# Cross-attention and ternary feed-forward: exponentials, reciprocal and normalisation of a unit each one slot later

## Chip, cores, metric

One core of one Trainium2 chip. The metric is the device time of one execution in microseconds (us).

## What is computed

The input x has 8 batches of 512 rows of 512 columns, the context 120 rows for each batch. All of it is float32 at the interface. Cut to what matters:

```python
x = x + xattn(layernorm(x), ctx, mask)      # 16 heads of 32; softmax over 120 keys; masked scores are 1e-9
x = x + ffn(layernorm(x))                   # two "bitlinear" layers, 512 -> 2048 -> 512, erf GELU between

def bitlinear(x, w, b):                     # rms-normalised rows rounded to 8-bit steps of the row's maximum,
    return act_quant(rmsnorm(x)) @ weight_quant(w).T + b      # weights rounded to -1, 0, 1
```

## The kernel before

Each engine runs its own instruction list, written out by hand, and the lists are tied by semaphores; every engine takes its list strictly in order. The work is cut into **units**: one unit is one group of 4 heads by 128 rows of one batch. A batch has 16 units (number u = 4 * head group + row tile), the kernel 128 (number n). All engines loop over **slots** n = 0 to 127 with a function `slot(n)` each, and in a slot each engine does its part of several units of different ages, with attention of batch a, projections for batch a + 1 and the feed-forward part of batch a - 1.

A unit's way through the attention, before the change:

- slot n, TensorE: `scores` (L416) into one of three PSUM banks ps_s, 128 rows by 480 columns (4 heads by 120 keys). It waits until the exponentials of unit n - 3 are done.
- slot n, VectorE: `softmax_max` puts 1e-9 at masked keys (L768) and takes the negated maximum per head (L771).
- slot n, ScalarE: `exps` (L626), 4 ACTIVATEs with Exp and the maximum as bias into prob (4 buffers); each also sums its row (the ACTIVATION_READ_ACCUMULATOR records).
- slot n + 1, VectorE: `invert_sums` (L776), the reciprocal of the 4 sums. GpSimd: `normalize` (L1024), prob times the reciprocal.
- slot n + 3 (LAG = 3), TensorE: `turn_probs` (L423), four transposes into one of two banks ps_t, which waits for `normalize` and for the bank's last reader. ScalarE: `evac_probs` (L601) copies them to probT.
- every 4 units, in slots with u = 3, 7, 11, 15: TensorE's `attend` (L434) multiplies with the values into the single bank ps_a; ScalarE's `evac_o` (L612) writes the rounded part oT_h, VectorE's `oT_low` (L740) the remainder oT_l. The next user of ps_a waits for it; in slot 3 that is the output projection (L366, 12 matmuls) of the batch before, which also needs its values; in slots 8 and 0 a query projection (also L366).

The feed-forward tile k (128 rows, 32 of them) takes 4 slots. TensorE's `ffn_up` (L453) fills ps_z, one quarter a slot, and VectorE's `evac_up` (L811) empties it into hid; the next quarter waits for that. In slots with u = 2, 6, 10, 14 (from unit 26 on) ScalarE's `gelu` (L633) runs over the full hid, a slot later its `square_h` (L639), then VectorE's `h_scale` (L817 to L823), then GpSimd's `round_h` (L1031, L1034) and `h_factor`; `ffn_down` (L463) and `evac_down` (L829) end it. GELU and Exp need different tables, so an ACT_TABLE_LOAD stands before the GELU and before the next Exp. In slots 6, 7, 10 and 11 GpSimd also rounds the feed-forward input (`round_x` L993 and L998, `y_factor`, `add_b2` L1019). Slots 11 to 13 turn the next batch's normalised input (L373) through ps_t, with a cast on ScalarE (L588) and a subtraction on VectorE (L735); slots 9 and 10 project the keys and values of the next batch (L396), copied by ScalarE (L617, L621); in slot 15 VectorE spreads the keys (`spread_keys`, L758).

Batch 0 also prepares the weights. In slot 0 ScalarE rounds wo (L673) and VectorE takes the remainder (L894). Slots 1 to 6 sum absolute values of 8 pieces of the two feed-forward weights (L648, L848). Slots 8 to 15 round a piece each (VectorE L855 and L858, GpSimd L1055 and L1058), and slots 9 to 16 turn it (L490): four groups of transposes, alternately into ps_z, emptied by ScalarE (L659), and ps_y, emptied by VectorE (L869); the third and fourth group wait for the evacuation of the first and second.

The order inside ScalarE's slot before: `evac_o`, `evac_probs(n - 3)`, `exps(n)`, then weights, evacuations of projections, `square_h`, `gelu`. VectorE's: residual, `evac_down`, `softmax_max(n)`, `spread_keys`, `invert_sums(n - 1)`, `oT_low`, `evac_up`, then weights, the layer norm statistics, `h_scale`. GpSimd's: `round_x`, `round_h`, `normalize(n - 1)`, `h_factor`, weights, `add_b2`, `add_bo`, `ln1_apply`.

Of the kernel before, what the change touches and what calls it, by code (L numbers as in the profile page):

```python
# [27 lines left out]
def xattn_bitffn_kernel(nc, x, ctx_in, mask, wq, bq, wk, bk, wv, bv, wo, bo, w1, b1, w2, b2, out):  # L28
# [19 lines left out]
    NU = NB * U  # L48
# [52 lines left out]
    with ExitStack() as stack:  # L101
# [483 lines left out]
        def _(act):  # L585
# [37 lines left out]
            def exps(n):  # L623
                wait(act, "sc_max", n + 1)
                for i in range(HG):
                    last = nc.scalar.activation(prob[:, n % 4, i * S2:(i + 1) * S2],  # L626
                                                ps_s[n % 3][:, i * S2:(i + 1) * S2], ACT.Exp,
                                                bias=nmax[:, n % 4, i:i + 1], accum_out=psums[:, n % 4, i:i + 1])
                last.then_inc(s["exp_done"], 1)
# [31 lines left out]
            def slot(n):  # L661
                a, u = divmod(n, U)
                more = a + 1 < NB
                if u == 3 and a > 0:
                    evac_o(a - 1, 3)
                if u in (7, 11, 15):
                    evac_o(a, u // 4 - 1)
                if n >= LAG:
                    evac_probs(n - LAG)
                exps(n)  # L670
                if n == 0:
                    act.wait_ge(s["wo_in"], 16)
                    nc.scalar.copy(wo_h[:], stage.rearrange("p (k n) -> p k n", k=KD)).then_inc(s["wo_high"], 1)  # L673
                if n in (1, 3, 5):
                    sum_abs(n + 1)
                if WTURN <= n < WTURN + 8:
                    evac_piece(n - WTURN, 0)
                    evac_piece(n - WTURN, 2)
                if u == 7 and more:
                    evac_ctx(a + 1)  # L680
                if u == 11 and more:
                    evac_xn(a + 1, 0)
                if u == 12 and more:
                    evac_xn(a + 1, 1)
                    evac_xn(a + 1, 2)
                if u == 13 and more:
                    evac_xn(a + 1, 3)
                k = tile_at(n, SQ0)
                if k is not None:
                    square_h(k)  # L690
                if u == 0:
                    evac_q(a, 1)
                if u == 1:
                    evac_q(a, 2)
                if u == 8:
                    evac_q(a, 3)
                if u == 14 and more:
                    evac_q(a + 1, 0)
                if u == 9 and more:
                    evac_keys(a + 1)  # L700
                if u == 10 and more:
                    evac_values(a + 1)
                k = tile_at(n, GELU0)
                if k is not None:
                    gelu(k)
# [13 lines left out]
            evac_values(0)  # L719
            for n in range(NU):  # L720
                slot(n)
            for n in range(NU - LAG, NU):
                evac_probs(n)
            evac_o(NB - 1, 3)
# [5 lines left out]
        def _(dve):  # L730
# [43 lines left out]
            def invert_sums(n):  # L774
                wait(dve, "exp_done", n + 1)
                v.reciprocal(pinv[:, n % 4], psums[:, n % 4]).then_inc(s["inv_ready"], 1)  # L776
# [48 lines left out]
            def evac_down(k):  # L825
                wait(dve, "x2b2_ready", k + 1)
                wait(dve, "hdeq_ready", k + 1)
                wait(dve, "y_full", k + 1)
                v.scalar_tensor_tensor(x2[:, k % XR], ps_y[:], h_deq[:, k % T:k % T + 1], x2[:, k % XR], ALU.mult,  # L829
                                       ALU.add).then_inc(s["y_evac"], 1)  # L830
# [40 lines left out]
            def slot(n):  # L871
                a, u = divmod(n, U)
                more = a + 1 < NB
                if u in (4, 5, 6, 7) and a > 0:
                    k = T * (a - 1) + u - 4
                    wo_done(k)
                    residual(k, ps_a)
                k = tile_at(n, YOUT0)
                if k is not None:
                    evac_down(k)  # L880
                softmax_max(n)
                if u == 15 and more:
                    spread_keys(a + 1)
                if n > 0:
                    invert_sums(n - 1)
                if u == 3 and a > 0:
                    oT_low(a - 1, 3)
                if u in (7, 11, 15):
                    oT_low(a, u // 4 - 1)
                if n >= UP0:  # L890
                    evac_up((n - UP0) // FC, (n - UP0) % FC, ps_z)
                if n == 0:
                    dve.wait_ge(s["wo_high"], 1)
                    v.tensor_tensor(wo_l[:], stage.rearrange("p (k n) -> p k n", k=KD), wo_h[:].bitcast(F32),  # L894
                                    ALU.subtract).then_inc(s["wo_split"], 1)
                if n in (2, 4, 6):
                    sum_abs(n + 1)
                if n == 7:
                    weight_scales()
                if WTURN <= n < WTURN + 8:  # L900
                    evac_piece(n - WTURN, 1)
                    evac_piece(n - WTURN, 3)
                if WROUND <= n < WROUND + 8 and dve_rounds(n - WROUND):
                    round_piece(n - WROUND)
                if u in (5, 6) and a > 0:
                    ln2_scales(T * (a - 1) + u - 5)
                if u in (9, 10) and a > 0:
                    ln2_scales(T * (a - 1) + u - 7)
                k = tile_at(n, ABS0)
                if k is not None:  # L910
                    h_scale(k)
                if u == 1 and more:
                    hide(a + 1, mask_in)
                if u in (1, 2) and more:
                    ln1_stats(a + 1, 2 * u - 2)
                    ln1_stats(a + 1, 2 * u - 1)
                if u == 11 and more:
                    xT_low(a + 1, 0)
                if u == 12 and more:
                    xT_low(a + 1, 1)  # L920
                    xT_low(a + 1, 2)
                if u == 13 and more:
                    xT_low(a + 1, 3)
# [16 lines left out]
            for n in range(NU):  # L940
                if n == 2 * U - 9:
                    dve.wait_ge(s["bias_in"], 48)
                slot(n)
            invert_sums(NU - 1)
            h_scale(25)
            for c in range(1, FC):
# [25 lines left out]
        def _(pool):  # L972
# [48 lines left out]
            def normalize(n):  # L1021
                wait(pool, "inv_ready", n + 1)
                pr = prob[:, n % 4].rearrange("p (h c) -> p h c", h=HG)
                gp.tensor_tensor(pr, pr, pinv[:, n % 4].unsqueeze(2).to_broadcast([P, HG, S2]), ALU.mult  # L1024
                                 ).then_inc(s["prob_ready"], 1)
# [35 lines left out]
            def slot(n):  # L1061
                a, u = divmod(n, U)
                more = a + 1 < NB
                if u == 6 and a > 0:
                    add_bo(T * (a - 1) + 3)
                if u in (6, 7) and a > 0:
                    round_x(T * (a - 1) + u - 6)
                    y_factor(T * (a - 1) + u - 6)
                if u in (10, 11) and a > 0:
                    round_x(T * (a - 1) + u - 8)  # L1070
                    y_factor(T * (a - 1) + u - 8)
                k = tile_at(n, QH0)
                if k is not None:
                    round_h(k)
                if n > 0:
                    normalize(n - 1)
                if k is not None:
                    h_factor(k)
                if WROUND <= n < WROUND + 8 and not dve_rounds(n - WROUND):
                    round_piece(n - WROUND)  # L1080
                if u in (6, 7) and a > 0:
                    add_b2(T * (a - 1) + u - 6)
                if u in (10, 11) and a > 0:
                    add_b2(T * (a - 1) + u - 8)
                if u == 2 and a > 0:
                    add_bo(T * (a - 1))
                    add_bo(T * (a - 1) + 1)
                if u == 3 and more:
                    ln1_apply(a + 1)
                if u == 4 and a > 0:  # L1090
                    add_bo(T * (a - 1) + 2)
# [9 lines left out]
            for n in range(NU):  # L1101
                if n == U + 2:
                    pool.wait_ge(s["bias_in"], 48)
                slot(n)
            normalize(NU - 1)
            round_h(25)
            h_factor(25)
# [43 lines left out]
```

## Time and profile before

| | |
|---|---|
| median of 3 runs | 857.52 us (854.35 to 858.08) |
| the profiled execution: its own time | 861.91 us |
| its span, first to last instruction | 860.1 us |
| TensorE matmul busy | 733.6 us, 85% |
| VectorE busy | 607.4 us, 71% |
| ScalarE busy | 536.8 us, 62% |
| GpSimd busy | 508.3 us, 59% |
| mean granted TensorE clock | 0.952 of full speed |

The numbers of the table below the first line are of one profiled execution. PE is TensorE, PEld its weight loads, DVE VectorE, ACT ScalarE, POOL GpSimd, SP SyncE. A row of the timeline gives start and duration in us, engine, line, operation, what it writes and reads, and in brackets how long the engine was idle before it and for whom it waited. The chain of waits is the chain of work that ended last, followed back from the end. Times of one instruction overlap a little with the next on the same engine.

### The profile page before, as it was taken

What the parts mean: (1) busy time and instruction counts of PE and PEld (TensorE: products, weight loads), DVE (VectorE), ACT (ScalarE), POOL (GpSimd) and SP (SyncE); (2) the same over time, 40 slices, a digit from 0 to 9 for tenths busy, and PEclk for the clock granted to TensorE, in tenths of its full rate; (3) what the DMA queues carried; (4) which work ended last, traced back from release to release, by engine and by line L of the source; (5) the groups of instructions that cost most, each with busy time, mean ns of one, the idle gap of its engine ahead of it and who ended that gap; (6) DMA issues with size and microseconds to landing.
All of it is one profiled execution on the core that took longest, in us unless ns stands there. A gap on an engine that the chain in (4) does not pass through costs nothing.

```text
span 860.1 us, 10519 instructions
## 1 busy us (share of the span) xinstructions
PE 733.6 (85%) x3213; PEld 423.7 (49%) x3266; DVE 607.4 (71%) x1069; ACT 536.8 (62%) x1448; POOL 508.3 (59%) x648
## 2 busy tenths in 40 slices
PE   1857858897999899998999899989998999879764
PEld 1434445553555455645565456545554556435221
DVE  4377456676778777877797687867787759858670
ACT  2357444457767786777766776777777776764230
POOL 3025233666478547864788458864785458776852
PEclk9977989998999999999999999999999999999897
DMA  9553251001422142224212231214223211232223
GB/s 312 179 191 125 100 187 53 25 19 26 125 52 43 43 135 61 50 49 134 61 38 57 78 98 49 56 30 127 57 49 50 74 50 49 50 94 59 68 74 86
DMA packets 111840, 70.17 MB, mean 82 GB/s; under 512 B 91368, under 2 KB 91368, under 8 KB 111016
## 3 DMA queue, kind: packets, MB, share of 16 engines
q1 hardware_dynamic: 110200, 69.48, 28.6%
q8 instruction: 27, 0.44, 0.2%
q10 hardware_dynamic: 1584, 0.01, 0.1%
q14 instruction: 29, 0.24, 0.1%
HBM read 40.11 MB, written 8.39 MB: 56 GB/s over the span
## 4 chain that ended last, share of the span: by engine, by line
PE 55%; DVE 18%; ACT 13%; POOL 6%; issue 4%; DMA 3%; DVEq 0%; SPq 0%; POOLq 0%; ACTq 0%
PE ps_a L366 18%; PE ps_z L453 8%; PE ps_s L416 7%; PE ps_y L463 7%; PE ps_a L396 6%; PE ps_t L423 4%; ACT prob L626 4%; DVE ps_s L768 3%; DVE nmax L771 3%; DVE hs L817 2%; ACT L633 2%; DVE kblk L758 2%; DMA q_hT<-q_h 2%; PE ps_a L434 2%; POOL hid L1031 1%
## 5 line engine op out<-in xcount | busy, mean ns | idle before, releaser
L1024 POOL TENSOR_TENSOR prob<-prob,pinv 128x480 f32<-128x480 f32 x128 | 128.1, 1001 | 225.1 <-DVE pinv L776 224.8
L626 ACT ACTIVATE prob<-ps_s,nmax 128x120 f32<-128x120 f32 x512 | 178.4, 366 | 48.1 <-DVE nmax L771 47.7
L601 ACT COPY probT<-ps_t 120x512 f32<-120x512 f32 x128 | 75.2, 588 | 111.6 <-PE ps_t L423 111.2
L463 PE MATMUL ps_y<-w2T,q_hT 128*128 128x512 bf16 x496 | 131.1, 392 | 15.2 <-DMA q_hT<-q_h 12.1
L768 DVE COPY_PREDICATED_SCALAR ps_s<-hidden_key,masked_c 128x480 f32 x128 | 91.6, 716 | 56.0 <-PE ps_s L416 54.9
L416 PE MATMUL ps_s<-kblk,qT 128*128 128x480 f32 x256 | 129.2, 588 | 2.1 <-DVE kblk L758 2.1
L453 PE MATMUL ps_z<-w1T,q_xT 128*128 128x512 bf16 x420 | 116.6, 395 | 9.3 <-DVE hid L811 6.8
L423 PEld LDWEIGHTS ps_t<-ident,prob 128*120 128x120 f32 x512 | 63.2, 144 | 102.9 <-issue 81.4
L626 ACT ACTIVATION_READ_ACCUMULATOR prob<-ps_s,nmax 128x1 f32 x512 | 108.0, 211 | 0.0
L423 PE MATMUL ps_t<-ident,prob 128*120 128x128 f32 x512 | 83.8, 289 | 24.1 <-DVE xnT_l L735 13.5
L1031 POOL TENSOR_SCALAR hid<-hid,hs 128x2048 f32<-128x2048 f32 x32 | 63.3, 1977 | 66.5 <-DVE hs L823 53.3
L811 DVE SCALAR_TENSOR_TENSOR hid<-ps_z,y_deq,b_row 128x512 f32<-128x512 f32 x114 | 83.2, 730 | 11.7 <-PE ps_z L453 11.4
L463 PEld LDWEIGHTS ps_y<-w2T,q_hT 128*128 128x128 bf16 x512 | 47.6, 100 | 80.6 <-issue 38.9
L771 DVE TENSOR_REDUCE nmax<-ps_s 128x4 f32<-128x480 f32 x128 | 84.2, 658 | 4.4
L639 ACT ACTIVATE q_h<-hid 128x2048 bf16<-128x2048 f32 x32 | 61.6, 1926 | 26.9 <-DMA q_hT<-q_h 26.9
L817 DVE TENSOR_REDUCE hs<-hid 128x1 f32<-128x2048 f32 x32 | 72.8, 2275 | 0.0
L633 ACT ACTIVATE hid<-hid 128x2048 f32<-128x2048 f32 x32 | 61.1, 1910 | 16.7 <-DVE hid L811 16.4
L453 PEld LDWEIGHTS ps_z<-w1T,q_xT 128*128 128x128 bf16 x456 | 45.0, 101 | 41.8 <-DVE hid L811 10.0
L1034 POOL TENSOR_SCALAR q_h<-hid 128x2048 bf16<-128x2048 f32 x32 | 60.8, 1899 | 2.8
L366 PE MATMUL ps_a<-wo_h,oT_h 128*128 128x512 f32 x116 | 50.3, 433 | 11.1 <-DVE oT_l L740 10.9
L366 PE MATMUL ps_a<-xnT_h,wq_h 128*128 128x512 f32 x128 | 57.4, 448 | 2.4 <-ACT qT L607 2.4
L829 DVE SCALAR_TENSOR_TENSOR x<-ps_y,h_deq,x 128x512 f32<-128x512 f32 x32 | 24.0, 749 | 49.7 <-PE ps_y L463 49.5
(130 smaller groups left out, 1375.6 us busy)
## 6 DMA issues: line engine op xcount, KB each, us to landing
hid<-in_L_ffn_w_dram SPq DMA_DIRECT2D x10, 1024.0 KB, 5.1
xn<-in_x_dram SPq DMA_DIRECT2D x8, 1024.0 KB, 6.1
x<-in_x_dram SPq DMA_DIRECT2D x32, 256.0 KB, 3.3
out_dram<-x SPq DMA_DIRECT2D x32, 256.0 KB, 2.2
x<-in_L_ffn_w_dram SPq DMA_DIRECT2D x3, 1024.0 KB, 5.0
ctx_k<-in_ctx_dram SPq DMA_DIRECT2D x8, 240.0 KB, 3.1
ctx_k<-in_mask_Bx1xSxS_ik_dram SPq DMA_DIRECT2D x7, 240.0 KB, 3.0
x<-in_L_xattn_wq_dram SPq DMA_DIRECT2D x1, 1024.0 KB, 8.9
```

The lines of the kernel that those rows point to most:

```text
L366: last = nc.tensor.matmul(bank, w, m, start=(k == 0 and i == 0), stop=(k == KD - 1 and i == 2))
L416: nc.tensor.matmul(ps_s[n % 3][:, 0:GK], qT[:, (G * a + g) % 3, t * P:(t + 1) * P], kblk[:, g], start=True, stop=True).then_inc(s["sc_full ...
L423: last = nc.tensor.transpose(bank[0:S2, i * P:(i + 1) * P], prob[:, n % 4, i * S2:(i + 1) * S2], ident[:])
L453: last = nc.tensor.matmul(bank[:], q_xT[:, k % 3, i], w1T[:, i, c * CH:(c + 1) * CH], start=(i == 0), stop=(i == KD - 1))
L463: last = nc.tensor.matmul(ps_y[:], q_hT[:, k % 2, f], w2T[:, f], start=(f == 0), stop=(f == KF - 1))
L626: last = nc.scalar.activation(prob[:, n % 4, i * S2:(i + 1) * S2], ps_s[n % 3][:, i * S2:(i + 1) * S2], ACT.Exp, bias=nmax[:, n % 4, i:i + ...
L633: nc.scalar.activation(hid[:, k % 2], hid[:, k % 2], ACT.Gelu).then_inc(s["gelu_done"], 1)
L768: v.copy_predicated(sc, hidden_key[:, a % 2, u % T].unsqueeze(1).to_broadcast([P, HG, S2]), masked_c[:].unsqueeze(2).to_broadcast([P, HG, ...
L771: v.tensor_reduce(out=nmax[:, n % 4], in_=sc, op=ALU.max, axis=AX_X, negate=True).then_inc(s["sc_max"], 1)
L811: v.scalar_tensor_tensor(hid[:, k % 2, c * CH:(c + 1) * CH], bank[:], y_deq[:, k % 8:k % 8 + 1], b1_row[:, c * CH:(c + 1) * CH], ALU.mult, ...
L817: v.tensor_reduce(out=hs[:, 3, t:t + 1], in_=hid[:, k % 2], op=ALU.max, axis=AX_X, apply_absolute_value=True).then_inc(s["h_abs"], 1)
L1024: gp.tensor_tensor(pr, pr, pinv[:, n % 4].unsqueeze(2).to_broadcast([P, HG, S2]), ALU.mult).then_inc(s["prob_ready"], 1)
```

## The change

Exponentials of unit n move from slot n to the head of slot n + 1 on ScalarE, ahead of `evac_o` and `evac_probs`. The reciprocal moves from slot n + 1 to slot n + 2 on VectorE, ahead of `softmax_max`. The normalisation moves from slot n + 1 to slot n + 2 on GpSimd, at its old place in the slot. The transposes stay in slot n + 3. After the loop the units left over are finished.

```diff
@@ ScalarE @@
             def slot(n):
                 a, u = divmod(n, U)
                 more = a + 1 < NB
+                if n > 0:
+                    exps(n - 1)
                 if u == 3 and a > 0:
                     evac_o(a - 1, 3)
                 if u in (7, 11, 15):
                     evac_o(a, u // 4 - 1)
                 if n >= LAG:
                     evac_probs(n - LAG)
-                exps(n)
...
             for n in range(NU):
                 slot(n)
+            exps(NU - 1)
             for n in range(NU - LAG, NU):
                 evac_probs(n)
@@ VectorE @@
                     evac_down(k)
+                if n > 1:
+                    invert_sums(n - 2)
                 softmax_max(n)
                 if u == 15 and more:
                     spread_keys(a + 1)
-                if n > 0:
-                    invert_sums(n - 1)
...
                 slot(n)
+            invert_sums(NU - 2)
             invert_sums(NU - 1)
             h_scale(25)
@@ GpSimd @@
                     round_h(k)
-                if n > 0:
-                    normalize(n - 1)
+                if n > 1:
+                    normalize(n - 2)
                 if k is not None:
                     h_factor(k)
...
                 slot(n)
+            normalize(NU - 2)
             normalize(NU - 1)
             round_h(25)
```

## Rows read from the trace of the kernel before

**Rows 1.** Busy time by stretch: us, PE, PEld, DVE, ACT, POOL busy (x instructions), PEclk, DMA share, GB/s
```profile
28.00:31.00 3.00, 2.11 (x6) 0.77 (x5) 0.00 (x0) 0.69 (x1) 0.00 (x0) 1.00 0.00 0
48.00:140.00 92.00, 64.59 (x293) 41.10 (x291) 57.28 (x92) 49.65 (x166) 33.55 (x29) 0.83 0.43 148
420.06:512.27 92.21, 86.27 (x387) 49.94 (x392) 71.87 (x131) 66.07 (x180) 61.14 (x79) 0.98 0.25 68
```

**Rows 2.** Waits, whole span: engine line <- releaser: us in total, times, longest us
```profile
POOL prob L1024 <- DVE pinv L776: 224.8, 63, 31.0
...
ACT prob L626 <- DVE nmax L771: 47.7, 74, 3.8
```

**Rows 3.** Timeline, slots 2 and 3 of batch 4: start us, us, engine line [idle before]
```profile
419.05 0.58 ACT L601 COPY probT<-ps_t 120x512 f32<-120x512 f32 x1 [1.43 <-PE ps_t L423]
...
420.03 0.72 DVE L811 SCALAR_TENSOR_TENSOR hid<-ps_z,y_deq,b_row 128x512 f32<-128x512 f32 x1
...
421.56 1.28 ACT L633 ACT_TABLE_LOAD   x1
...
422.85 1.91 ACT L633 ACTIVATE hid<-hid 128x2048 f32<-128x2048 f32 x1
...
424.67 0.67 ACT L612 ACTIVATE oT_h<-ps_a,bv_col 128x512 fp32r<-128x512 f32 x1
...
425.37 0.75 DVE L740 SCALAR_TENSOR_TENSOR oT_l<-ps_a,bv_col,oT_h 128x512 fp32r<-128x512 f32 x1 [0.93 <-ACT oT_h L612]
...
426.27 0.47 PE L366 MATMUL ps_a<-wo_h,oT_h 128*128 128x512 f32 x1 [1.42 <-DVE oT_l L740]
```

**Rows 4.** Timeline, slot 15 and 0 after it
```profile
495.96 0.67 ACT L612 ACTIVATE oT_h<-ps_a,bv_col 128x512 fp32r<-128x512 f32 x1
...
498.71 0.74 DVE L811 SCALAR_TENSOR_TENSOR hid<-ps_z,y_deq,b_row 128x512 f32<-128x512 f32 x1
...
499.51 1.04 PE L453 MATMUL ps_z<-w1T,q_xT 128*128 128x512 bf16 x4
```

**Rows 5.** Timeline, slots 11 to 13
```profile
476.94 0.69 DVE L735 TENSOR_TENSOR xnT_l<-ps_t,xnT_h 128x512 fp32r<-128x512 f32 x1 [2.33 <-ACT xnT_h L588]
...
482.89 1.11 PE L423 MATMUL ps_t<-ident,prob 128*120 128x128 f32 x4 [2.09 <-DVE xnT_l L735]
```

**Rows 6.** Timeline, GpSimd in slot 7, TensorE in slot 8
```profile
451.23 0.99 POOL L1024 TENSOR_TENSOR prob<-prob,pinv 128x480 f32<-128x480 f32 x1
...
451.68 0.60 PE L423 MATMUL ps_t<-ident,prob 128*120 128x128 f32 x4
```

**Rows 7.** Timeline, last unit's reciprocal
```profile
764.52 0.18 DVE L776 RECIPROCAL pinv<-psums 128x4 f32<-128x4 f32 x1 [1.85 <-ACT prob L626]
```

**Rows 8.** Timeline, slot 10 of batch 0
```profile
89.02 0.58 ACT L617 COPY ctx_k<-ps_a 120x512 f32<-120x512 f32 x1 [4.88 <-PE ps_a L396]
...
91.28 0.36 ACT L626 ACTIVATE prob<-ps_s,nmax 128x120 f32<-128x120 f32 x1 [0.43 <-DVE nmax L771]
...
92.63 0.61 ACT L659 ACTIVATE w2T<-ps_z 128x512 bf16<-128x512 f32 x1
...
93.29 0.58 PE L490 MATMUL ps_z<-ident,hid 128*128 128x128 f32 x2 [2.20 <-ACT w2T L659]
```

**Rows 9.** Chain of waits, unit 0 and on
```profile
42.48 1.79 ACT wo_h L673
...
44.29 2.30 DVE wo_l L894
...
47.00 5.32 DMA ctx_k<-in_mask_Bx1xSxS_ik_dram
```

**Rows 10.** Chain of waits, two output projections
```profile
157.35 4.58 PE ps_a L366 x12
...
426.27 3.00 PE ps_a L366 x12
```

**Rows 11.** Timeline, the first of the two
```profile
157.35 0.47 PE L366 MATMUL ps_a<-wo_h,oT_h 128*128 128x512 f32 x1 [2.39 <-DVE oT_l L740]
```

## The prediction

> **What bounds the kernel now.** I read the busy time by stage first [rows 1]. One batch of 16 units in the middle takes 92.21 us and TensorE is busy 86.27 of them: TensorE is the bound there, and only some 6 us a batch are left in which it waits. In the stretch that turns the weights (48 to 140) TensorE is busy only 64.59 of 92.00 us: there it waits for other engines. Next the list of waits [rows 2]: the one that the change is made for, ScalarE's exponentials waiting for VectorE's negated maximum, is 47.7 us in 74 places. A wait of ScalarE is not yet time of the kernel. So I then went through the timeline of one middle batch and of the start and asked at each TensorE gap what ScalarE did before it [rows 3]. In the middle TensorE waits in few places, each time behind a short chain that runs through ScalarE: the evacuation of an attention group (L612), its low half on VectorE (L740), and then either the output projection, or the evacuation of ps_z (L811) that stands behind L740 in VectorE's queue.
>
> **The change, part by part.** No instruction is added or taken away and no DMA is moved (SyncE's queue waits for the same events as before). Exponentials, reciprocal and normalisation of a unit move one slot later. What counts is the new order in three first-in-first-out queues. On ScalarE one unit's exponentials now stand ahead of L612 and of the copy of the turned probabilities (L601). From their start to that of the next instruction it is 1.35 us (91.28 to 92.63, [rows 8]). In slots 3, 7, 11 and 15 a GELU was the last thing on ScalarE, so the load of the exponential table (1.28 us, as the GELU's own in [rows 3]) moves ahead of L612 with them: 2.8 us in all stand ahead of L612 that stood behind it.
>
> *Slot 3 (output projection, batches 2 to 7).* Before: copy 419.05, exponentials 420.06 after VectorE's maximum, table load 421.56, GELU 422.85, L612 424.67, L740 425.37, TensorE 426.27 [rows 3]. After: exponentials of the older unit lie in the 1.43 us that ScalarE waited before its copy, so the load can start at 419.64 and the GELU at 420.93; its last input starts at 420.03 and takes 0.72, so it is there. Then: load 422.86, exponentials 424.16, L612 425.52. It is 0.85 late against 424.67, though the GELU was 1.9 early. Six times: **+5.1**.
>
> *Slot 15 to 0 (six passages, from batch 1 to 2 on).* The GELU doesn't start earlier here, as a projection of TensorE ends before it, so L612, at 495.96 before, is put back by the full 2.8, to 498.73. VectorE spreads the keys meanwhile, which hides half of it: L740 0.70 later at 499.43 as in [rows 3], ps_z evacuated behind it from 500.10 instead of 498.71, and TensorE, which took ps_z at 499.51 [rows 4], is 1.4 late. Six times: **+8.4**.
>
> *Slot 11 to 12 (batches 1 to 6).* Here a chain of ScalarE's cast and VectorE's subtraction of the next input holds TensorE already; VectorE sat idle 2.33 us in it, TensorE 2.09 at its end [rows 5]. The late L612 lands in that idle time; L740 and L811 then run directly before the subtraction and put it back by 0.3. Six times: **+1.8**.
>
> *Slot 7.* L612 had waited for TensorE and the GELU is early, so it is late by 0.3 only, 3 us before anybody needs it: nothing; the cover is those 3 us.
>
> *GpSimd.* Its first wait of its own list (224.8 us for the reciprocal, [rows 2]) shrinks, which is worth nothing where it idled. But the unit that TensorE turns in slot n+1 is now normalised in slot n, behind rounding work of that slot. I compared for all 16 slots the end of the normalisation in slot n with TensorE's transposes of slot n+1: it holds by 0.6 to 4 us, except in slot 7, where GpSimd has a queue of feed-forward work without a pause: 451.23 + 0.99 is 452.22, the transposes began at 451.68 [rows 6]. Late by 0.6 with the semaphore, batches 2 to 7: **+3.6**.
>
> *Last batch.* TensorE has light slots and the chain goes through ScalarE and VectorE. The same 2.8 us in slot 11 put back VectorE's next evacuation of ps_z by 2.0; at the end two sets of exponentials, one load and the GELU lie in front of the reciprocal, which waited 1.85 for them at 764.52 [rows 7]: that one becomes some 3.8 late, and the rest of the tail hangs on it. **+3.8**. Ends: 0 to 6.
>
> *Weights being turned (units 9 to 16).* This is what the change gains. In slot 10: ScalarE copied keys at 89.02 (0.58), waited for the maximum, did exponentials at 91.28, evacuated ps_z at 92.63, and TensorE went on at 93.29 after 2.20 idle [rows 8]. After: exponentials directly at 89.60, copy 91.08, evacuation 91.67, TensorE 92.33: 0.95 earlier. The same steps in slots 9 to 16 give 1.4, 0.95, 1.0, 1.4, 1.9, 1.6, 0.2, 1.8 (in slot 15 VectorE's key spreading takes over as the limit): **-10.2**. Ends: -6 (a weight piece or GpSimd's rounding late) and -14 (no low clock).
>
> *Start.* wo had landed before 28 (no DMA traffic from 28 to 31, [rows 1]), yet its cast stood behind unit 0's exponentials and ran at 42.48, then VectorE's split 44.29, then the mask's load 47.00, which held VectorE [rows 9]. The cast now comes first, so the split can begin at 41.0: 3.3 earlier. Some is lost later, as GpSimd's layer norm now stands ahead of the normalisation that the first attention needs: **-2.2**, ends 0 and -5.
>
> *Clock.* The gap in slot 3 grows from 1.42 to 2.27 us. After such a gap (2.39 us, batch 1, [rows 11]) the same 12 matmuls took 4.58 us instead of 3.00 [rows 10]: they ran at the lower clock, as TensorE does in slot 12, where its four transposes take 1.11 us [rows 5] instead of 0.60 [rows 6]. Nothing at one end; 1.8 at each of 12 gaps (slots 3 and 0), so 21.6, at the other. The gap of slot 3 is nearly that of batch 1, the one of slot 0 is shorter, so I take half of the first six: **+5.4**.
>
> Losses 5.1 + 8.4 + 1.8 + 3.6 + 3.8 = 22.7, start -12.4, clock +5.4: **+15.7 us**. The profiled execution took 861.9 (span 860.1), 4.4 over the median of 857.5, so 877.6 on its scale and 873.2 for the median.
>
> A rule that speaks against the change: [rows 3] show a table load of 1.28 us and the GELU beginning 1.29 after the load began. The Trainium skill, "ScalarE: Activation LUTs", section "What ACT_TABLE_LOAD costs", adds a drain of about 1380 ns to every switch, 2.66 us in all. By it, each of the 14 moved switches (slots 3 and 15, tail) would cost 1.38 more and the sum would be +35. The trace disagrees with it here.
>
> **Rivals.**
> (a) The forecast, the clock falling at some gaps: 867 to 881, likeliest 873.2. 55%.
> (b) The clock does not fall more often: 857.5 + 10.3 = 867.8. 14%. For it: a gap of 1.42 left the projection at 3.00 [rows 10].
> (c) It falls at all 12: 857.5 + 10.3 + 21.6 = 889.4. 11%.
> (d) Faster: the coupling of maximum and exponentials is the whole cause of TensorE's idle time in the start, 92.0 - 64.6 = 27.4 us [rows 1], while the losses are as above: 857.5 + 22.7 - 27.4 = 852.8. It decides if unit 16 begins over 27 us earlier. Against it: I can point at 12.4 only; the rest waits for DMA, for VectorE's rounding and for GpSimd. 11%.
> (e) Hardly anything: the GELU is early by as much as L612 is put back, so slots 3 and 15 and the tail cost nothing, and the start gives only 2.2: 857.5 + 1.8 + 3.6 - 2.2 = 860.7. In half of the slots ScalarE did not wait for the maximum at all (74 waits for 128 units, [rows 2]). Against it: the GELU's input arrives at 420.75. 7%.
> (f) A moved table switch costs twice its row, because ScalarE's pipe has to empty where other work now stands in front: 14 times 1.29 on (a), 891. The rows show no such time: 2%. That is about what the Trainium skill, "ScalarE: Activation LUTs", would give.
>
> **How the numbers follow.** Half a per cent, 4.3 us, is about what a measurement of this kernel can tell from no change. Slower by more than that: (a), (b), (c), (f), 0.82. Within: (e), 0.07. Faster: (d), 0.11. The range leaves out (d), (e) and (f), 20%, and reaches from 861 (b with the largest gain at the start) to 890 (c).
>
> **What would show it.** In the profile of after: the wait of L626 for L771 is nearly gone; L612 in slots 3, 11 and 15 follows a table load and exponentials; TensorE's wait for L740 in a middle batch is above 2 us, and before ps_z in slot 0 there is a new one of about 1.5; a batch takes some 95 to 97 us instead of 92.2; unit 16 starts about 12 us earlier; TensorE waits for L1024 in slot 8. A batch that stays at 92 us would make the prediction wrong, and so would a start that gains over 20 us.

## The result, and the profile after

The changed kernel takes 873.91 us (median of 4 runs, 872.36 to 877.05) against 857.8 for the kernel before on the same chip: 1.0186 times as long, 95% interval 1.0145 to 1.0228. The forecast was 873.2. The profiled execution has a span of 875.2 us against 860.1, so 15.1 us are to be found. VectorE's L-numbers are 2 higher in the new kernel (L771 is now L773, L740 is L742, L811 is L813) and GpSimd's are 3 higher (L1024 is L1027); those of TensorE and ScalarE up to L673 are the same.

The wait that the change was made to remove is down to a third, and others are there. This is the list of waits of the changed kernel (engine, line, what it waited for: us in total, times, longest); the first line answers to the second of [rows 2]:

```profile
ACT prob L626 <- DVE nmax L773: 15.2, 20, 4.7
...
POOL prob L1027 <- DVE pinv L778: 203.5, 48, 33.5
...
PE ps_t L423 <- POOL prob L1027: 25.7, 17, 5.1
...
PE ps_z L453 <- DVE hid L813: 17.8, 15, 3.4
...
PE ps_a L366 <- DVE oT_l L742: 15.5, 7, 2.3
```

ScalarE's wait for the maximum fell from 47.7 us in 74 places to 15.2 in 20; 6.0 of these stand at 52 and 57 us, at the first units. TensorE's waits rose: for the normalisation in total to 25.7 us in 17 places (10.2 in 3 before), for ps_z to 17.8 (6.8), for oT_l before the projection to 15.5 (10.9).

Where the time went is best read from one instruction that each unit has once, VectorE's negated maximum. Its start, after against before, is a clock for the whole kernel. Timeline rows for unit 16, the changed kernel, then unit 120:

```profile
122.66 0.66 DVE L773 TENSOR_REDUCE nmax<-ps_s 128x4 f32<-128x480 f32 x1
...
733.46 0.66 DVE L773 TENSOR_REDUCE nmax<-ps_s 128x4 f32<-128x480 f32 x1
```

In the kernel before the same two start at:

```profile
140.66 0.66 DVE L771 TENSOR_REDUCE nmax<-ps_s 128x4 f32<-128x480 f32 x1
...
728.77 0.66 DVE L771 TENSOR_REDUCE nmax<-ps_s 128x4 f32<-128x480 f32 x1
```

So unit 16 comes 18.0 us earlier, unit 120 4.7 us later. With unit 24 (before at 180.40, after at 160.14), read in the same way, the 15.1 us are: **-20.3** up to unit 24, **+25.0** from unit 24 to unit 120, **+10.4** from there to the end.

These numbers are of one execution of each kernel. s7 below runs the same code as the change up to unit 112, and its trace shows how far two executions differ: it is 21.9 us ahead of the kernel before at unit 24 (the change 20.3) and 0.4 ahead at unit 112 (the change 3.8 behind). The distance inside one slot repeats from batch to batch within 0.03 us where the granted clock is the same.

**The middle.** Busy time by stretch of the same batch as in [rows 1] (unit 64 to unit 80; columns as there):

```profile
401.52:497.14 95.62, 87.09 (x394) 49.87 (x393) 71.62 (x130) 65.74 (x181) 60.97 (x80) 0.98 0.24 66
```

95.62 us instead of 92.21 (the same stretch between units 64 and 80 before is 92.20), with about the same work done by every engine. The difference comes in four steps, each seen where the distance between the two kernels' maxima changes: 0.88 between slots 3 and 4, 0.62 between 8 and 9, 0.43 between 11 and 12, 1.47 between 15 and 0; together 3.4. The first, in the changed kernel's timeline, answers to [rows 3]:

```profile
412.60 0.59 ACT L601 COPY probT<-ps_t 120x512 f32<-120x512 f32 x1
...
413.21 1.28 ACT L633 ACT_TABLE_LOAD   x1
...
413.50 0.74 DVE L813 SCALAR_TENSOR_TENSOR hid<-ps_z,y_deq,b_row 128x512 f32<-128x512 f32 x1
...
414.50 1.91 ACT L633 ACTIVATE hid<-hid 128x2048 f32<-128x2048 f32 x1
...
416.43 1.28 ACT L626 ACT_TABLE_LOAD   x1
...
417.72 0.36 ACT L626 ACTIVATE prob<-ps_s,nmax 128x120 f32<-128x120 f32 x1
...
419.08 0.70 ACT L612 ACTIVATE oT_h<-ps_a,bv_col 128x512 fp32r<-128x512 f32 x1
...
419.82 0.75 DVE L742 SCALAR_TENSOR_TENSOR oT_l<-ps_a,bv_col,oT_h 128x512 fp32r<-128x512 f32 x1 [1.90 <-ACT oT_h L612]
...
420.71 0.47 PE L366 MATMUL ps_a<-wo_h,oT_h 128*128 128x512 f32 x1 [2.31 <-DVE oT_l L742]
```

ScalarE copies at 412.60, the table load follows at once, and the GELU starts when the load has ended (414.50); its last input, L813, was there at 414.24. Then come table load (416.43), exponentials (417.72) and only then L612 (419.08). TensorE sits idle 2.31 us where it was 1.42. The passage from slot 15 to 0 answers to [rows 4]:

```profile
494.27 0.70 ACT L612 ACTIVATE oT_h<-ps_a,bv_col 128x512 fp32r<-128x512 f32 x1
...
495.00 0.75 DVE L742 SCALAR_TENSOR_TENSOR oT_l<-ps_a,bv_col,oT_h 128x512 fp32r<-128x512 f32 x1 [1.65 <-ACT oT_h L612]
...
495.67 0.74 DVE L813 SCALAR_TENSOR_TENSOR hid<-ps_z,y_deq,b_row 128x512 f32<-128x512 f32 x1
...
496.47 1.04 PE L453 MATMUL ps_z<-w1T,q_xT 128*128 128x512 bf16 x4 [1.55 <-DVE hid L813]
```

Here a wait of TensorE for ps_z of 1.55 us is new. In slot 8 it is GpSimd ([rows 6] before):

```profile
445.58 0.98 POOL L1027 TENSOR_TENSOR prob<-prob,pinv 128x480 f32<-128x480 f32 x1
...
446.71 0.62 PE L423 MATMUL ps_t<-ident,prob 128*120 128x128 f32 x4 [0.45 <-POOL prob L1027]
```

**The start.** The same stretches of 10 us in both kernels, by engine and clock (they do not hold the same work, as the changed kernel is ahead); first the changed one:

```profile
80.00:90.00 10.00, 9.08 (x37) 5.08 (x36) 5.17 (x7) 3.54 (x12) 1.92 (x3) 1.00 0.47 173
...
90.00:100.00 10.00, 8.72 (x65) 6.22 (x64) 6.80 (x12) 7.95 (x26) 5.74 (x4) 1.00 0.39 143
```

and the kernel before:

```profile
80.00:90.00 10.00, 7.77 (x27) 4.29 (x26) 2.21 (x6) 3.15 (x11) 4.84 (x3) 0.83 0.33 105
...
90.00:100.00 10.00, 7.80 (x29) 4.57 (x26) 4.98 (x7) 3.61 (x12) 0.98 (x1) 0.83 0.31 105
```

TensorE has more to do in the same time, and its granted clock is 1.00 where it was 0.83. The same can be read slot by slot, from the maximum of unit n to that of unit n + 1. These are slots 9, 10, 12 and 13 of the changed kernel:

```profile
76.45:84.01 7.56, 6.55 (x31) 3.87 (x30) 2.75 (x6) 3.54 (x14) 5.27 (x4) 1.00 0.37 139
84.01:91.57 7.56, 6.64 (x31) 3.03 (x29) 5.17 (x7) 3.54 (x14) 1.68 (x2) 1.00 0.38 139
97.19:104.35 7.16, 4.08 (x31) 3.27 (x30) 6.26 (x9) 4.54 (x15) 0.99 (x2) 1.00 0.73 250
104.35:108.83 4.48, 3.31 (x22) 2.12 (x21) 3.33 (x7) 3.14 (x13) 4.31 (x4) 1.00 0.27 75
```

and of the kernel before:

```profile
80.06:90.58 10.52, 8.29 (x32) 4.80 (x31) 2.73 (x5) 3.46 (x12) 4.84 (x3) 0.84 0.31 100
90.58:101.10 10.52, 8.32 (x31) 4.15 (x29) 5.16 (x7) 3.41 (x12) 0.98 (x1) 0.84 0.29 100
108.03:117.75 9.72, 5.62 (x30) 4.74 (x30) 6.25 (x9) 4.25 (x13) 0.99 (x1) 0.82 0.52 190
117.75:125.27 7.52, 5.13 (x26) 3.98 (x25) 3.43 (x7) 3.54 (x13) 4.83 (x3) 0.77 0.23 76
```

In slots 11, 14, 15 and 16 the clock is 1.00 in both. Slot 10 of batch 0 answers to [rows 8]:

```profile
82.45 0.59 ACT L617 COPY ctx_k<-ps_a 120x512 f32<-120x512 f32 x1 [3.27 <-PE ps_a L396]
...
82.93 0.37 ACT L626 ACTIVATE prob<-ps_s,nmax 128x120 f32<-128x120 f32 x1
...
84.28 0.61 ACT L601 COPY probT<-ps_t 120x512 f32<-120x512 f32 x1
...
84.75 0.64 ACT L659 ACTIVATE w2T<-ps_z 128x512 bf16<-128x512 f32 x1
...
85.45 0.66 PE L490 MATMUL ps_z<-ident,hid 128*128 128x128 f32 x4 [0.92 <-ACT w2T L659]
```

The wait for L659 is 0.92 instead of 2.20 us. But the whole slot (maximum of unit 10 to that of unit 11) fell from 10.52 to 7.56, by more than that wait. The rest, 1.7 us, is nearly all TensorE's speed: from the third group of transposes (L490) to the start of the value projection it is 0.93 us instead of 1.66, and the projection (L396, 8 matmuls) takes 3.45 instead of 4.34.

**The end.** GpSimd in slot 125 and TensorE in slot 126, among the light slots of the last batch:

```profile
760.97 1.97 POOL L1034 TENSOR_SCALAR hid<-hid,hs 128x2048 f32<-128x2048 f32 x1 [4.24 <-DVE hs L825]
...
763.03 1.90 POOL L1037 TENSOR_SCALAR q_h<-hid 128x2048 bf16<-128x2048 f32 x1
...
764.89 0.98 POOL L1027 TENSOR_TENSOR prob<-prob,pinv 128x480 f32<-128x480 f32 x1
...
766.02 1.08 PE L423 MATMUL ps_t<-ident,prob 128*120 128x128 f32 x4 [3.52 <-POOL prob L1027]
```

GpSimd normalises unit 123 only after `round_h` (1.97 and 1.90 us), and TensorE sits idle 3.52 us for it. The four transposes behind the gap take 1.08 us, in slot 8 above 0.62: the granted clock of this slot is 0.63. It takes 9.2 us, where it took 2.9 at a clock of 1.00 before.

### The profile page after: what moved, and what is told of

It is laid out like the page before. It is cut to its first block, busy times and chain, and to the rows that moved or that the text cites. A ratio compares the mean times of both kernels' runs of the same rounds, so it can differ in the third digit from the quotient of the medians.

```text
span 875.2 us, 10572 instructions
## 1 busy us (share of the span) xinstructions
PE 737.0 (84%) x3266; PEld 420.1 (48%) x3266; DVE 604.1 (69%) x1069; ACT 533.3 (61%) x1448; POOL 506.1 (58%) x648
## 4 chain that ended last, share of the span: by engine, by line
PE 37%; POOL 22%; ACT 18%; DVE 14%; issue 6%; DMA 3%; ACTq 0%; SPq 0%; DVEq 0%; POOLq 0%
PE ps_a L366 13%; PE ps_a L396 6%; PE ps_z L453 5%; ACT hid L633 4%; DVE hs L819 4%; POOL hid L1034 4%; PE ps_s L416 4%; POOL q_h L1037 4%; ACT prob L626 4%; PE ps_y L463 3%; PE ps_t L423 3%; POOL prob L1027 3%; ACT L626 3%; ACT L633 3%; DVE hid L813 2%
## 5 line engine op out<-in xcount | busy, mean ns | idle before, releaser
L1027 POOL TENSOR_TENSOR prob<-prob,pinv 128x480 f32<-128x480 f32 x128 | 126.9, 992 | 203.7 <-DVE pinv L778 203.5
L626 ACT ACTIVATE prob<-ps_s,nmax 128x120 f32<-128x120 f32 x512 | 178.7, 371 | 15.5 <-DVE nmax L773 15.2
L463 PE MATMUL ps_y<-w2T,q_hT 128*128 128x512 bf16 x512 | 136.8, 399 | 11.2 <-DMA q_hT<-q_h 11.2
L453 PE MATMUL ps_z<-w1T,q_xT 128*128 128x512 bf16 x456 | 123.2, 394 | 17.8 <-DVE hid L813 17.8
L601 ACT COPY probT<-ps_t 120x512 f32<-120x512 f32 x128 | 76.5, 599 | 87.6 <-PE ps_t L423 85.4
L423 PEld LDWEIGHTS ps_t<-ident,prob 128*120 128x120 f32 x512 | 61.4, 143 | 126.5 <-issue 95.3
L423 PE MATMUL ps_t<-ident,prob 128*120 128x128 f32 x512 | 84.0, 289 | 44.2 <-POOL prob L1027 25.7
L626 ACT ACTIVATION_READ_ACCUMULATOR prob<-ps_s,nmax 128x1 f32 x512 | 110.5, 216 | 0.0
L813 DVE SCALAR_TENSOR_TENSOR hid<-ps_z,y_deq,b_row 128x512 f32<-128x512 f32 x114 | 84.8, 744 | 24.0 <-PE ps_z L453 24.0
L773 DVE TENSOR_REDUCE nmax<-ps_s 128x4 f32<-128x480 f32 x128 | 84.2, 657 | 4.4
L607 ACT ACTIVATE qT<-ps_a,bq_col 128x512 f32<-128x512 f32 x32 | 22.0, 688 | 75.9 <-PE ps_a L366 75.9
L366 PE MATMUL ps_a<-wo_h,oT_h 128*128 128x512 f32 x116 | 51.1, 441 | 15.6 <-DVE oT_l L742 15.5
L742 DVE SCALAR_TENSOR_TENSOR oT_l<-ps_a,bv_col,oT_h 128x512 fp32r<-128x512 f32 x32 | 24.0, 750 | 55.3 <-ACT oT_h L612 55.3
```

The lines of the kernel that those rows point to most:

```text
L366: last = nc.tensor.matmul(bank, w, m, start=(k == 0 and i == 0), stop=(k == KD - 1 and i == 2))
L423: last = nc.tensor.transpose(bank[0:S2, i * P:(i + 1) * P], prob[:, n % 4, i * S2:(i + 1) * S2], ident[:])
L453: last = nc.tensor.matmul(bank[:], q_xT[:, k % 3, i], w1T[:, i, c * CH:(c + 1) * CH], start=(i == 0), stop=(i == KD - 1))
L463: last = nc.tensor.matmul(ps_y[:], q_hT[:, k % 2, f], w2T[:, f], start=(f == 0), stop=(f == KF - 1))
L813: v.scalar_tensor_tensor(hid[:, k % 2, c * CH:(c + 1) * CH], bank[:], y_deq[:, k % 8:k % 8 + 1], b1_row[:, c * CH:(c + 1) * CH], ALU.mult, ...
```

## The experiments

All ratios are to the kernel before in the same session (859.6, 858.6 and 859.5 us for the three sessions). A number "a batch" is the stretch from unit 64 to unit 80, as above. Every distance at a unit or at the end is read against the one trace of the kernel before. That execution took 861.9 us, among the longest of this kernel (854.6 to 862.0 in these sessions, the longer ones at the lower mean clock: 0.952 at 862.0, 0.963 at 854.7). So a gain of the span comes out larger than that of the medians: 19.9 against 15.7 us in s4, 26.6 against 24.4 in s9. The first four tell the places of the loss and the gain apart.

**s1: the exponentials one slot back, but at their old place in the slot.**

```diff
-                if n > 0:
-                    exps(n - 1)
...
                 if n >= LAG:
                     evac_probs(n - LAG)
+                if n > 0:
+                    exps(n - 1)
```

> The change, but ScalarE does the exponentials of the unit one slot back at their old place in the slot, behind L612 and L601. My theory (the cost in the middle is that exponentials and a table load stand ahead of L612): the start still gains 18 to 20 us, the late evacuations in slots 3, 11 and 15 are gone (a batch of about 92 us or less, as the GELU is early and the gap of slot 3 can close), GpSimd's lateness in slot 8 and in the last batch stays: 840 to 850 us. Rival (it is the longer way of a unit, one slot more between scores and transposes, whatever the order): a batch stays at 95.6 us and the time at 868 to 874.

Measured: 862.26 us, 1.0032 (1.0011 to 1.0053). A batch takes 92.29 us, so the loss of the middle is a matter of the order inside ScalarE's slot and not of the longer way of a unit; that part of the rival is out. But the time missed my 840 to 850. The start gained only 12.3 us by unit 16 and not 18: behind the copy L601 the exponentials wait for TensorE's transposes again (ScalarE's waits for them at L601 from 75 to 142 us sum to 9.4 in 8 places), and slot 15 has a granted clock of 0.83. And the last 8 units and the tail lost 9.7 us, as in the change.

**s2: the change, with GpSimd's normalisation first in its slot.**

```diff
+                if n > 1:
+                    normalize(n - 2)
                 if u == 6 and a > 0:
                     add_bo(T * (a - 1) + 3)
...
-                if n > 1:
-                    normalize(n - 2)
```

> The change, but GpSimd normalises first in its slot, ahead of the rounding work. My theory (TensorE waits for L1027 in slot 8 and in the last batch because the normalisation stands behind rounding): 0.6 us a batch comes back and most of the tail's 10 us, so about 864 us, with TensorE's wait for L1027 down from 25.7 us to the start's share. Rival (GpSimd is as late with the rounding, and that is on the path): 871 to 876.

Measured: 864.94 us, 1.0080 (1.0052 to 1.0109), as the theory had it, yet only in part for its reason. From unit 120 to the end it loses 2.8 us instead of 10.4: that is the normalisation behind `round_h`. Most of what is left of the gain is that batch 2 takes 94.86 us instead of 98.20, because in this execution the clock did not fall there; that has nothing to do with the edit. In the middle a batch still takes 95.42 us: the step of 0.6 in slot 8 went, and one of about as much came between slots 5 and 6, where the residual additions that GpSimd prepares are now late (TensorE waits 0.4 us for L783 before the attention matmuls). There the rival was right. The stretch also shows the clock at work: it falls in slot 3 (the 12 matmuls of the output projection take 4.58 us) and then not in slots 12 and 13, where it fell in the kernel before, and the two cancel within 0.02 us.

**s3: ScalarE's part alone.** Reciprocal and normalisation as before, `exps(n - 1)` at the head of the slot.

> Only ScalarE's part of the change; reciprocal and normalisation stay one slot after the scores, as before. My theory (the parts are independent: gain at the start and loss in slots 3, 11, 0 are ScalarE's, slot 8 and part of the tail are GpSimd's): start gain near 20 us, a batch of about 95.0 us (92.2 + 0.88 + 0.43 + 1.47), about 862 to 867 us. Rival (VectorE now waits for the exponentials in front of ps_z's evacuation in each slot, as the reciprocal stands ahead of L811): batches above 96 us, 875 or more.

Measured: 876.12 us, 1.0198 (1.0142 to 1.0255); span 876.6. The start gains the same (18.0 by unit 16, 19.6 by unit 24). The middle is worse than in the change: batches take 97.3 to 99.0 us. The steps in slots 3, 11 and 0 are there, the one in slot 8 is not, and two new ones of 1.0 and 1.4 stand behind slots 12 and 13. The first comes with TensorE's wait for the next input's low part, 2.1 us instead of 1.1 in the change. That fits the rival: the reciprocal now waits for exponentials done in the same slot, and L737 and L813 are behind it. The second is the clock, which neither side had: slot 13 takes 6.2 us at a granted clock of 0.60 where the change takes 4.7 at 0.79, and in batches 2 and 5, where it is 0.82, this step is 0.6 and -0.2 us. The longest batch, 99.0 us, has a fall in slot 3 as well (4.59 us for the projection). So leaving the reciprocal and the normalisation at their old places costs this ScalarE order 1.7 us a batch in all (97.3 against 95.6); the two were not moved one by one. The tail lost 3.2.

**s4: the late exponentials only in slots 1 to 24**, everything else as before.

```diff
+    EARLY = 24
+                if 0 < n <= EARLY:
+                    exps(n - 1)
...
-                exps(n)
+                if n >= EARLY:
+                    exps(n)
```

> The kernel before, with the exponentials one slot late only in slots 1 to 24 (both units' in slot 24), reciprocal and normalisation as before. My theory (the gain is all in the start, the losses all after unit 24): the start gains 18 to 20 us and the batches take 92.2 us: 837 to 841 us, faster than both kernels. Rival (the start's gain needs the reciprocal and the normalisation late as well, or is given back where the order changes over): 850 to 858.

Measured: 843.88 us, **0.9832 (0.9789 to 0.9875)**, some 3 us over the forecast's upper end in the median, 19.9 us less in span (840.2). The forecast was worked out in spans, and the medians give 15.7. A batch takes 92.19 us. The gain sits in the first 24 slots (19.5 us by unit 24), needs ScalarE's order alone, and is not given back.

The next four ask what exactly costs the middle and the end, and what the start's gain is made of.

**s5: the change, with the exponentials behind L612 and L601 in slots 3, 7, 11 and 15 from unit 27 on.**

```diff
-                if n > 0:
+                if n > 0 and not (n > GELU0 and u % 4 == 3):
                     exps(n - 1)
...
+                if n > GELU0 and u % 4 == 3:
+                    exps(n - 1)
```

> The change, but in the slots that follow a GELU (3, 7, 11, 15 from unit 27 on) the exponentials, and so the table load, stand behind L612 and L601. My theory (the steps of 0.88, 0.43 and 1.47 us a batch in slots 3, 11 and 0 come from these 2.8 us in front of L612 and L601 and from nothing else): start gain 20 us as in the change, batches of 95.6 - 2.8 = 92.8 us, 850 to 857 us. Rival (a unit's way is too long by a slot wherever the exponentials stand): batches near 95 us, 865 or more.

Measured: 844.06 us, 0.9837 (0.9808 to 0.9867), better than forecast. Batches take 91.1 to 91.6 us, less than in the kernel before; the tail still loses 8.8 us. Its timeline in slot 3:

```profile
401.05 0.67 ACT L612 ACTIVATE oT_h<-ps_a,bv_col 128x512 fp32r<-128x512 f32 x1
...
402.21 1.28 ACT L626 ACT_TABLE_LOAD   x1
...
402.55 0.74 DVE L744 SCALAR_TENSOR_TENSOR oT_l<-ps_a,bv_col,oT_h 128x512 fp32r<-128x512 f32 x1
...
403.44 0.47 PE L366 MATMUL ps_a<-wo_h,oT_h 128*128 128x512 f32 x1 [0.31 <-DVE oT_l L744]
```

L612 comes right behind the GELU, the table load after it, and TensorE's gap of 1.42 us is down to 0.31. This is the 1.9 us by which the prediction had the GELU earlier, now without anything in front of L612 to spend it. Only 1.1 of it reach TensorE, as VectorE takes L744 (the old L740) behind its maximum at 402.55.

**s6: only L612 ahead of the exponentials, in all slots.**

```diff
-                if n > 0:
-                    exps(n - 1)
...
+                if n > 0:
+                    exps(n - 1)
                 if n >= LAG:
                     evac_probs(n - LAG)
```

> The change, but with L612 ahead of the exponentials; only L601 stays behind them. My theory (slots 3 and 0 pay through L612 alone, slot 11 through L601, the copy that frees a bank for TensorE's transposes): batches of about 93.2 us, start gain 20 us, 853 to 860 us. Rival (the late copy L601 is what holds TensorE, L612 only looks so): batches of 95 us or more, 866 to 874.

Measured: 848.84 us, 0.9905 (0.9877 to 0.9932). A batch takes 91.27 us, so the late L612 was nearly all of the middle's loss: leaving L601 behind the exponentials costs nothing visible there. The 0.43 of slot 12 did not stay (0.06), so my attribution of it to L601 in this expectation was wrong. The passage from slot 15 to 0 costs 0.2 instead of 1.5. By unit 16 the start gained 15.9, in s5 18.4.

**s7: the change, with the normalisation first in the slot for the last batch alone.**

> The change, but in the last batch alone GpSimd normalises ahead of its rounding. My theory (in the last batch's light slots TensorE waits for the normalisation behind round_h, 3.5 us at once in slot 14, which the prediction left out): 7 to 8 us back of the 10 that the last 8 units and the tail lose, 865 to 868 us, all batches before as in the change. Rival (the tail is long because of ScalarE's and VectorE's lists alone): 872 to 875.

Measured: 866.31 us, 1.0100 (1.0070 to 1.0130). A batch takes 95.55 us, as in the change; unit 120 comes 1.0 us later than before and the end 4.0. So from unit 120 on 3.0 us are lost instead of 10.4: the order on GpSimd is worth 7.4 us in the last batch, with the clock that goes with it (1.00 in slot 126, 0.63 in the change). Before unit 112 this kernel is the change, and yet the clock did not fall once in its slots 3 and 0 of batches 2 to 7.

**s8: the kernel before, with the transposes of the second group of each weight piece issued four times over** (the same data to the same place).

```diff
-                    for c in range(4):
+                    for c in [c for _ in range(4 if q == 1 else 1) for c in range(4)]:
```

> The kernel before, with the second group of weight transposes (into ps_y, slots 9 to 16) issued four times over, same data into the same place, so that TensorE works where it waited for ScalarE's L659. It adds 1.3 us of TensorE work to each slot at the high clock. Theory (a third of the start's gain is the clock: TensorE ran slots 9 to 14 partly at the lower one because it idled behind the exponentials): no lower clock between 80 and 125 us, the key and value projections take 3.4 us instead of 4.6 and 4.3, unit 16 starts 2 to 5 us earlier than before, 853 to 857 us. Rival (the clock is not the cause): projections unchanged, unit 16 starts 0 to 5 us later, 858 to 863 us.

Measured: 857.33 us, 0.9984 (0.9965 to 1.0004), the difference to the kernel before is not resolved by the times and lies between the two forecasts. The trace shows the parts. Stretches of 10 us:

```profile
80.00:90.00 10.00, 8.35 (x46) 5.43 (x44) 3.54 (x6) 4.90 (x18) 5.25 (x4) 1.00 0.29 107
...
90.00:100.00 10.00, 9.44 (x53) 5.71 (x54) 6.02 (x8) 4.34 (x14) 2.90 (x2) 1.00 0.34 105
```

and from its chain of waits the two projections, which took 4.63 and 4.34 us before:

```profile
82.40 3.43 PE ps_a L396 x8
...
91.24 3.43 PE ps_a L396 x8
```

With TensorE kept busy in the gap the granted clock stays at 1.00 there. It doesn't in slot 13, so "no lower clock between 80 and 125 us" failed:

```profile
112.05:119.23 7.18, 6.83 (x44) 6.12 (x43) 3.44 (x7) 3.80 (x13) 4.83 (x3) 0.80 0.17 40
```

Unit 16 starts at 134.63, 6.0 us earlier than before, but 1.5 of these are there at unit 9, before the first added transpose; 4.6 belong to the edit, though each of the 8 slots has 12 transposes more and the exponentials still wait for the maximum. Slots 9 and 10 alone give 3.4. So in these slots idle time costs twice: itself, and the lower clock of what follows. About 1.2 us of it is lost again up to unit 24, and the end is 3.5 us earlier in the profiled execution, 1.3 in the medians.

**s9: all three put together.** s5 up to unit 117, from there the order of the kernel before on ScalarE, VectorE and GpSimd: on VectorE and GpSimd (not shown in the cut) the calls for unit n - 2 run while n <= TURN, those for n - 1 from n >= TURN on.

```diff
+    TURN = 117
+                if 0 < n <= TURN and not (n > GELU0 and u % 4 == 3):
+                    exps(n - 1)
...
+                if GELU0 < n <= TURN and u % 4 == 3:
+                    exps(n - 1)
+                if n >= TURN:
+                    exps(n)
...
```

> The order of s5 (exponentials a slot late, but behind L612 and L601 in the slots after a GELU) up to unit 117, and the order of the kernel before in the last 11 units, on all three engines. My theory (start, middle and tail are separate terms that add): start gain 20 us, batches of 91.1 us, and a tail that loses 1 us instead of 8.8, so 844 - 7.5, about 836 to 839 us, faster than s4 and s5. Rival (the change-over in slot 117 or a late GELU gives it back, or the tail is long for what came before it): 842 to 846.

Measured: 835.09 us (833.5 to 836.06, 5 runs), **0.9713 (0.9690 to 0.9735)**. Unit 24 comes 21.8 us earlier, unit 120 26.0, the end 26.6: the tail loses nothing. The terms add about as forecast (836 to 839), and this version is faster than both kernels.

## Why the prediction was right

It said +15.7 us, and it is 15.1 in span and 16.1 in the medians. Between units 24 and 120 it said 23.7 and 25.0 were measured, and the mechanism of that loss was right; the whole sum came out because two large errors outside this stretch cancel. By its own steps:

- *Slot 3*, 0.85 predicted, 0.88 measured a batch. The rows of the changed kernel go through the same instructions, load, exponentials, L612, at the same distances (from the copy to L612 6.47 us predicted, 6.48 measured). s5 and s6, which take the exponentials from in front of L612, remove it. Shown.
- *Slot 15 to 0*, 1.4 predicted, 1.47 measured, 2.36 at the first of the six passages. s6, with L612 alone ahead, leaves 0.2 of it. Shown.
- *Slot 11 to 12*, 0.3 predicted, 0.43 measured. It is gone in s6, where only L612 goes ahead, so it is L612 and the VectorE work queued behind its low half, as the prediction had it: counted from the maximum of unit 11, the subtraction (L735, now L737) starts at 5.73 us in the kernel before and in s6, and at 6.10 in the change, where L742 and L813 stand directly in front of it. Shown.
- *Slot 7 to 8*, 0.6 predicted for GpSimd, 0.62 measured between slots 8 and 9. s2 shows the place: with the normalisation in front the step leaves slot 8, and the same amount turns up in slot 6. With both orders that were tried on GpSimd it is lost somewhere.
- *Clock in the middle*, 5.4 predicted (three falls of 1.8). It fell twice at these 12 gaps, both in batch 2: the query projection of slot 0 took 4.35 us instead of 2.8 and the output projection of slot 3 4.57 instead of 3.0, so 3.1 us.

```profile
208.61 4.35 PE ps_a L366 x12
...
229.00 4.57 PE ps_a L366 x12
```

  In the other batches the same gaps of 1.55 and 2.31 us left the clock alone. The price of 1.8 was too high: [rows 10] give 1.58. And the number of falls is no property of the change: s7, the same code up to unit 112, has none, s2 has five and s3 four at the same places. So "I take half of the first six" was a guess, and that it fits is luck.
- *Table load*: the changed kernel begins the load 0.02 us after the GELU's end and the exponentials 1.29 after that, with the load now behind a long ACTIVATE. Nothing beyond the load's own row is to be seen; rival (f) is out by the trace of after.

Two terms were mis-sized by more, and they cancel:

- *The start*, -12.4 predicted, -20.3 measured by unit 24. The failing step is "The same steps in slots 9 to 16 give 1.4, 0.95, ...": it took every other duration over from the trace of before. Slot by slot it reads:

| slot | 9 | 10 | 11 | 12 | 13 | 14 | 15 | 16 |
|---|---|---|---|---|---|---|---|---|
| predicted gain, us | 1.4 | 0.95 | 1.0 | 1.4 | 1.9 | 1.6 | 0.2 | 1.8 |
| measured gain, us | 2.96 | 2.96 | 1.31 | 2.56 | 3.04 | 1.36 | 0.20 | 1.86 |
| clock before | 0.84 | 0.84 | 1.00 | 0.82 | 0.77 | 1.00 | 1.00 | 1.00 |
| clock after | 1.00 | 1.00 | 1.00 | 1.00 | 1.00 | 1.00 | 1.00 | 1.00 |

  In the four slots where the clock was 1.00 already the steps hold within 0.3 us. In the four where it was lower 5.9 us are missing: their durations held TensorE at the lower clock, and the clock came back when the gap shrank. Even the end "-14 (no low clock)" was too small, the eight slots gave 16.3. s8 shows the mechanism by itself, in the old order and with more work for TensorE: slots 9 and 10 are 3.4 us shorter at the clock of 1.00, which is about the 3.6 that the prediction lacks there. (Its working for slot 10 also puts 1.48 us between exponentials and copy, 89.60 to 91.08, where its own row gives 1.35; that changes the step by 0.1.)
- *The last batch*, +4.4 predicted with its share of slot 8, +10.4 measured. The failing step is "I compared for all 16 slots": I compared them in a middle batch, where a slot is 4.3 to 7.2 us long, and carried the result to the last batch, whose last slots take 2.0 to 2.9. There 3.9 us of `round_h` in front of the normalisation cannot be covered, and the clock falls behind the gap. s7 gives 7.4 us of it back. The 3.0 that it leaves, and the 3.2 that s3 loses with GpSimd's order unchanged, are near the 3.8 that the prediction had for ScalarE and VectorE.

So the time was right by luck with both errors in it; as a forecast of the parts it was 7.9 and 6.0 us off. By its own sign "a start that gains over 20 us" would have made it wrong, and the start gained 18.0 us by unit 16, for which it had said 12, and 20.3 by unit 24. One more sign came half true: ScalarE's wait for the maximum was to be nearly gone and is 15.2 of 47.7 us.

## What to carry to other kernels

When a wait is removed by doing a step one slot later, the place inside the slot decides more than the slot: here the same delay costs 1.9% at the head of ScalarE's slot everywhere and gains 1.6% when, in the four slots of a batch that follow a GELU, it stands behind the evacuation that TensorE waits for (s5). Look for the stage where the coupling is the bound and change the order there alone; a middle with 6 us of idle TensorE in 92 has little to win and much to lose. And check a slack in each stage with its own slot length: what holds in a slot of 6 us fails in one of 3. Where a wait that goes leaves TensorE busier, ask what the clock was: durations read at 0.8 of full speed are not those of the kernel after.

## What the runs showed of the hardware

I had not expected TensorE's clock to carry so much of the gain. In the weight stage the granted clock was 0.83 of full speed in two stretches of 10 us in the kernel before and 1.00 in the changed one, and redundant transposes in an idle gap of some 2 us (s8) were more than paid for up to unit 16 by the higher clock of the matmuls after it; over the whole kernel the times resolve no gain. The same gap does not always do the same: after one of 2.31 us the output projection took 3.0 us in five batches and 4.57 in one, and in s2, with the same gap, 3.0 in three and 4.6 in three. Nor does a fall cost the same everywhere: in s5 three of the batches 3 to 6 have none in slots 12 and 13, where the kernel before had one; slot 13 is 1.5 us shorter there, and TensorE then waits 0.9 us for the normalisation in slot 14, so that a batch gains 0.4 to 0.5 by it.
